# One-hot rows with the compared columns innermost in a four-layer graph network on one core

## The reference

```python
x = _layernorm(x + _L0_gnn_ref(x, src, dst, L0_gnn_W), axis=-1)      # mean over incoming edges
x = _layernorm(x + _L1_gnn_ref(x, edge_index, ...), axis=-1)         # sums over 16 neighbours of each node, twice
x = _layernorm(x + _L2_gnn_ref(x, ...), axis=-1)                     # attention over the edges
x = _layernorm(x + _L3_gnn_ref(batch0, src, dst, x, ...), axis=-1)

# in _L1: the neighbours of each node after a sort, deg = 16
order = jnp.lexsort((nbr, nodes))
nbrs = nbr[order].reshape(N, deg)
for k in range(deg):
    out = out + w[1 + k] * h[nbrs[:, k]]

# in _L3: how often each node is the source of an edge
deg_out = jax.ops.segment_sum(ones_e, src, num_segments=n)
norm_src = jax.lax.rsqrt(jnp.maximum(deg_out, 1.0))
```

## Time and profile before

| what | value |
|---|---|
| median of three runs | 10770.39 us |
| the profiled execution | 10772.08 us, of which 10770.3 us are the span of the profile |
| PE, DVE, ACT, POOL busy | 78%, 72%, 59%, 68% |
| the degree count (L564, L584, L587, L599) | ends at 512.7 us |
| mean layer and sort | about 540 to 2700 us |
| first window of layer 1 | about 2900 to 5540 us |
| second window of layer 1 | about 5550 to 6990 us |
| attention, last layer | 7000 us to the end |

### The profile page before, as it was taken

One profiled execution on the slowest core, in us unless ns is written; L12 is line 12 of the kernel. 1 busy time (PEld: TensorE's weight loads), 2 busy tenths in 40 slices (PEclk: granted clock), 3 DMA queues, 4 the chain that ended last, 5 costly groups with the idle time before them and its releaser, 6 DMA issues.

```text
span 10770.3 us, 189635 instructions
## 1 busy us (share of the span) xinstructions
PE 8431.4 (78%) x45271; PEld 6636.6 (62%) x45271; DVE 7796.5 (72%) x26977; ACT 6315.6 (59%) x18928; POOL 7356.1 (68%) x7060
## 2 busy tenths in 40 slices
PE   3344555555788999888889999989999999948987
PEld 2233444444466776677777878767777777736765
DVE  5678656655866777565654446788888888899999
ACT  6877777776856666111100004677777777756665
POOL 0076777777088888888838888466666666639995
PEclk6555555555889999999999999955555555557776
DMA  2021222222678888999967775221111111110000
GB/s 48 1 74 47 52 53 53 53 53 56 216 198 204 217 218 213 261 250 246 252 228 228 233 226 122 34 71 46 46 46 46 46 46 46 46 44 1 1 1 25
DMA packets 656017, 1170.97 MB, mean 109 GB/s; under 512 B 140942, under 2 KB 565074, under 8 KB 632158
## 3 DMA queue, kind: packets, MB, share of 16 engines
q0 software_dynamic: 363536, 437.35, 21.2%
q10 hardware_dynamic: 25344, 574.83, 13.9%
q1 hardware_dynamic: 266062, 146.67, 5.4%
HBM read 885.82 MB, written 278.99 MB: 108 GB/s over the span
## 4 chain that ended last, share of the span: by engine, by line
POOL 32%; DVE 19%; PE 18%; issue 14%; ACT 12%; DVEq 3%; DMA 2%; SPq 1%; ACTq 0%; POOLq 0%
POOL step_data L1404 12%; POOL onehot L2091 8%; PE bank L1365 7%; POOL step_data L1676 7%; POOL gather_ring L1404 4%; DVE step_small L1911 2%; DVE keys L1051 2%; ACT keys L584 2%; ACT onehot L980 2%; PE bank L1951 2%; DVE keys L1060 2%; PE bank L991 2%; ACT onehot L978 2%; DVE arena L1024 2%; PE bank_tile L1959 1%
## 5 line engine op out<-in xcount | busy, mean ns | idle before, releaser
L966 POOL DMA_INDIRECT gather_ring<-mean_rows,step_data x1660 | 1593.2, 960 | 951.3 <-DVE arena L763 396.9
L991 PE MATMUL bank<-gather_ring,onehot 128*128 128x130 f32 x3320 | 1045.6, 462 | 1050.8 <-DVE arena L1024 728.2
L1365 PE MATMUL bank<-arena 128*128 128x384 bf16 x9506 | 1796.6, 329 | 26.6 <-DMA arena<-split_out 24.8
L1365 PE MATMUL bank<-arena,keys 128*128 128x384 bf16 x9408 | 1791.6, 330 | 9.3 <-DMA arena<-split_im 9.3
L1404 POOL DMA_INDIRECT step_data<-hidden,window_idx x960 | 1554.9, 1620 | 315.9 <-issue 291.5
L991 PEld LDWEIGHTS bank<-gather_ring,onehot 128*128 128x128 f32 x3320 | 811.7, 309 | 1274.0 <-issue 853.5
L1365 PEld LDWEIGHTS bank<-arena 128*128 128x128 bf16 x9506 | 1306.9, 138 | 328.1 <-issue 39.8
L1365 PEld LDWEIGHTS bank<-arena,keys 128*128 128x128 bf16 x9408 | 1294.2, 138 | 317.8 <-issue 34.5
L1676 POOL DMA_INDIRECT step_data<-next_rows,window_idx x672 | 1117.3, 1663 | 343.7 <-issue 314.6
L1882 POOL DMA_INDIRECT gather_ring<-attention_rows,step_data x834 | 786.1, 943 | 606.7 <-DVE step_small L1935 459.5
L1882 POOL DMA_INDIRECT keys<-attention_rows,step_data x826 | 778.4, 942 | 468.3 <-DVE step_small L1935 420.3
(11 more groups left out here) (361 smaller groups left out, 22016.6 us busy)
## 6 DMA issues: line engine op xcount, KB each, us to landing
keys<-count_rows ACTq DMA_DIRECT2D x56, 3136.0 KB, 11.6
arena<-count_rows ACTq DMA_DIRECT2D x56, 3136.0 KB, 11.4
count_rows<-arena ACTq DMA_DIRECT2D x29, 3136.0 KB
count_rows<-keys ACTq DMA_DIRECT2D x29, 3136.0 KB
gather_ring<-mean_rows,step_data POOLq DMA_INDIRECT x1660, 2.5
step_data<-hidden,window_idx POOLq DMA_INDIRECT x960
gather_ring<-attention_rows,step_data POOLq DMA_INDIRECT x834, 2.5
keys<-attention_rows,step_data POOLq DMA_INDIRECT x826, 2.5
```

Source lines behind the costliest of these rows:

```text
L966: e.indirect_dma_start(ring_at(rings.slot(name, i), SUM_COLS, SUMS - 1), None, rows, bass.IndirectOffsetOnAxis(src_idx[:, i:i + 1], 0), bo ...
L991: e.matmul(pass_bank[i % N_SUM_BANKS][:, 0:SUMS], onehot[:, i % STEP_SLOTS, :], ring_at(rings.slot(name, i), SUM_COLS, SUMS), start=True, ...
L1365: m = e.matmul(pass_bank[n % 2][:, 0:SPLIT_COLS], counts[t % 2][:, :, h], split[:, h, :], start=(h == 0), stop=(h == NODE_TILES - 1))
```

## The change

Both kinds of one-hot tables turn their two inner dimensions: the column (or group) is now the innermost one. What was `[slot][column][value]` is `[slot][value][column]`, and `low_hot` goes from `[group][value]` to `[value][group]`. For this the comparison needs an iota in which each value stands 8 or 4 times in a row: `iota_wide` (128 x 8) and `iota_quad` (128 x 4), two copies made once at the start. In the comparison before, the digits were an operand whose innermost step is 0 (one digit repeated 98 or 128 times). Now the digits run innermost with step 1 and are repeated by an outer dimension, and the iota is read plainly. The results of a comparison are written as one contiguous run, as before.

The other users of the tables now step through them. ACT's eight writes of a group (L584) go to every eighth element, 16 bytes apart, and PE reads both operands of the degree count with that step. For the count matrices, PE reads its stationary operand in steps of 4 elements, 8 bytes. ACT's relu still runs over all 1024 elements at once.

Last, `far` names 1 group out of 4 rather than 3 out of 5, which makes 50 groups of low one-hots on ACT rather than 120, and 150 on DVE rather than 80. All of ACT's groups (0, 4, 8, ...) now lie in slot 0 of the ring.

```diff
+    iota_quad = sb("iota_quad", [P, P, HOT_GROUPS], BF16)
...
     low_hot = [onehot[:, 4 + 2 * i:6 + 2 * i, :].rearrange("p s e -> p (s e)").bitcast(BF16).rearrange(
-        "p (g e) -> p g e", e=P) for i in range(2)]
+        "p (e g) -> p e g", g=HOT_GROUPS) for i in range(2)]
...
-        "p (s c w) -> p s c w", s=HIST_SLOTS, c=HIST_COLS) for at, w in ((0, NODE_TILES), (2 * LANE // 4, P)))
+        "p (s w c) -> p s w c", s=HIST_SLOTS, c=HIST_COLS) for at, w in ((0, NODE_TILES), (2 * LANE // 4, P)))
+    iota_wide = acc[:, 60 * P:60 * P + P * HIST_COLS // 2].bitcast(BF16).rearrange("p (w c) -> p w c", c=HIST_COLS)
...
     def far(i):
-        return i % 5 in (0, 2, 4)
+        return i % 4 == 0
...
                 e.tensor_tensor(to[:, s, :, :],
-                                of[:, cols].rearrange("p (c o) -> p c o", o=1).to_broadcast(
-                                    [LOAD_PARTS, HIST_COLS, width]),
-                                iota_half[0:LOAD_PARTS, 0:width].rearrange("p (o w) -> p o w", o=1).to_broadcast(
-                                    [LOAD_PARTS, HIST_COLS, width]), ALU.is_equal).then_inc(made)
+                                of[:, cols].rearrange("p (o c) -> p o c", o=1).to_broadcast(
+                                    [LOAD_PARTS, width, HIST_COLS]),
+                                iota_wide[0:LOAD_PARTS, 0:width, :], ALU.is_equal).then_inc(made)
...
-                    e.activation(to[:, c, :], iota_half[0:LOAD_PARTS, :], ACT.Abs, bias=low_digit[:, at:at + 1],
+                    e.activation(to[:, :, c], iota_half[0:LOAD_PARTS, :], ACT.Abs, bias=low_digit[:, at:at + 1],
                                  scale=-1.0).then_inc(hist_far)
...
-                m = e.matmul(hist, low_store[:, s, c, :], high_store[:, s, c, :], start=(i == c == 0),
+                m = e.matmul(hist, low_store[:, s, :, c], high_store[:, s, :, c], start=(i == c == 0),
...
+        own().tensor_copy(iota_wide[:, :, :], iota_half[:, :].rearrange("p (w o) -> p w o", o=1).to_broadcast(
+            [P, P, HIST_COLS])).then_inc(n.sem, n.up())
+        own().tensor_copy(iota_quad[:, :, :], iota_half[:, :].rearrange("p (w o) -> p w o", o=1).to_broadcast(
+            [P, P, HOT_GROUPS])).then_inc(n.sem, n.up())
...
-                low_code[t % 2][:, g:g + HOT_GROUPS].rearrange("p (c o) -> p c o", o=1).to_broadcast([P, HOT_GROUPS, P]),
-                iota_half[:, :].rearrange("p (o w) -> p o w", o=1).to_broadcast([P, HOT_GROUPS, P]),
+                low_code[t % 2][:, g:g + HOT_GROUPS].rearrange("p (o c) -> p o c", o=1).to_broadcast([P, P, HOT_GROUPS]),
+                iota_quad[:, :, :],
                 ALU.is_equal).then_inc(lows_made)
...
-        e.matmul(count_bank[b % 4][:, 0:GROUP_COLS], low_hot[c % 2][:, i, :], high_hot[b >= ROUND][c % 2][:, i, :],
+        e.matmul(count_bank[b % 4][:, 0:GROUP_COLS], low_hot[c % 2][:, :, i], high_hot[b >= ROUND][c % 2][:, i, :],
```

## The result

The changed kernel takes 10706.8 us (median of four runs, 10704.28 to 10712.14), against 10770.15 (median of four, 10768.21 to 10776.99) on the same chip: a ratio of 0.9941, with a 95% interval of 0.9923 to 0.9958. It is 63 us faster. Forecast were 171 us and a time of 10599. The direction was right, the size was not, and the time lies above the range of 10560 to 10690.

A forecast was written before the change was run, and what follows sets the result against it. ACT was taken to bound the degree count, gathers the first window of layer 1. Savings of 151 us (count) and 20 us (gathers) made 171 us, so 10599 us; forecast 10565 to 10635, range 10560 to 10690.

The forecast's parts named there:

- What bounds the kernel: Degree count: ACT alone is the chain, 99.3%, with serial work behind; layer 1's first window: gathers; DVE bounds neither window.
- DVE's durations: Comparisons of 784, 1024 and 512 elements were to take about 0.56, 0.68 and 0.43 us.
- The lower end: New DVE comparison: 0.52 ns an element, from one-source rows of 4-byte elements; the upper end was today's 1.042.
- The edge-row loop: Degree count's start, taken to hang on DVE: 16.6 us less, so ACT's next group starts at 154.0 us.
- The turn: Degree count: ACT's group and PE's matmuls in series, 5.13 us per four groups; 40 turns, count ends at 361.3 us.
- Two costs of it no row shows directly: 16-byte steps in the degree count: ACT's write +40 ns an Abs, PE's read +25 ns a matmul.
- the steps bind: Rival: 16-byte writes and reads cost their upper ends, turn 6.65 us, 111 us less, 10659 us; chance 0.22.
- DVE doesn't get faster: Rival: comparisons stay at 1.042 ns an element, DVE bounds the degree count, 49 us less, 10721 us; chance 0.06.
- The slower case: Rival: the quick comparison holds up layer 1's gathers more, 26 us slower in all, 10796 us; chance 0.04.
- The gathers: First window of layer 1: shorter comparison cuts gather delays of at most 54 us by 38%; 20 us taken.
- PE's weight load: Count matrices: stationary operand's load may grow from 98 to 138 ns, hidden behind matmuls of 384 columns; price 0.

The follow-up runs named there:

- e4: Changed kernel, but PE reads both operands of the degree count as contiguous runs (counts come out wrong): 11244.94 us, count to 438.6 us.
- e11: Changed kernel with 8-byte steps as in e2, and ACT making the low one-hots of 1 group in 5: 11191.95 us, 0.9822 of the kernel before.
- e2: Changed kernel with all low one-hots on DVE and a group's columns in two blocks of four (8-byte steps): 11145.95 us, 0.9822 of the kernel before.
- e5: Kernel before with the count-matrix part alone (low_hot turned, iota_quad): 11320.51 us, 0.9977 of the kernel before.
- e7: Kernel before with the count-matrix part alone, plus a memset of 240 elements behind each low comparison: 11316.74 us, 0.9979 of the kernel before.
- e8: Kernel before with the new share alone (far names 1 group in 4), old layouts: 11292.75 us, 0.9954 of the kernel before.
- e1: Changed kernel, but DVE makes all low one-hots of the degree count and ACT none: 11205.27 us, 0.9876 of the kernel before.
- e9: Changed kernel, but PE reads only the stationary operand of the degree count contiguously (counts come out wrong): 11325.02 us, count to 481.4 us.
- e3: Changed kernel, but each ACT Abs writes 128 elements in a row (source degrees come out wrong): 11200.38 us, count to 395.8 us.
- e6: Kernel before with the count-matrix part alone, each low comparison made twice: 11332.46 us, 0.9989 of the kernel before.
- e10: Changed kernel, but PE reads only the moving operand of the degree count contiguously (counts come out wrong): 11297.06 us, count to 446.4 us.

## Why the prediction went wrong

**What bounds the kernel**: right. ACT alone paced the degree count, and nothing hides behind it: ACT's, PE's and DVE's share there changed and the rest moved along (mean layer 2147 us in both).

**DVE's durations**: right. 566, 685 and 425 ns were measured, about 560, 680 and 430 forecast. The lower end (0.52 ns an element, from the 4-byte rows) was the one to take: from 784 to 1024 elements it is now (685 - 566) / 240 = 0.50 ns an element, where it was 1.042. With this the trace agrees with both halves of the rule on two 16-bit tensors in the Trainium skill, "VectorE: DVE Perf Modes", section "Mode 2×_1P".

**The edge-row loop**: wrong by 10.2 us. I let it hang on DVE (16.6 us less), but a PE group of 1.45 us instead of 0.65 fills its rounds: 24 matmuls and three transposes are 5.4 of 5.9 us. In e4, with contiguous reads, ACT's first group after the loop starts at 155.4 us, near my 154.0; in the changed kernel at 164.16.

**The turn**: the failed step. Its form held (first Abs to relu's end, to PE, to the free slot). The passage "Two costs of it no row shows directly" chose +40 ns an Abs and +25 ns a matmul, with ends of +172 and +82. Measured were (4.97 - 2.43) / 8 = +318 ns and +100 ns: beyond both upper ends. The turn is therefore 2.22 us longer by ACT and 0.60 by PE than forecast, 7.94 instead of 5.13. The sum over 40 turns is 112 us; with the 10.2 of the loop and the 3.0 that are left for the tail, where PE's last three groups take 1.45 us each, not 0.7, it is the whole gap between 361.3 and 486.8 us.

What was wrong in the reasoning is that I read the cost as one that grows slowly with the length of the step, and placed 16 bytes near 8 because it is far from 196 and 528. The runs show a steep rise between 8 and 16 bytes instead:

| step of 2-byte elements | eight Abs of 128 (write) | distance of matmuls, 98 columns (moving read) |
|---|---|---|
| contiguous | 2.43 to 2.45 us | 81 to 83 ns |
| 8 bytes | 2.63 us (e11) | 91 ns (e11), 0.89 us for eight (e2) |
| 16 bytes | 4.83 to 4.97 us | 175 to 181 ns |

The sentence of the Trainium skill, "Advanced Engine Details and Errata", section "SBUF Cachelines", that I quoted against my sum (lines of 16 bytes, a penalty for a new line at every access) also says that at least two hits on a line are needed to absorb the latency. A step of 8 bytes gives two hits, one of 16 gives one. The table agrees with that on both sides. No run has a step between 8 and 16 bytes or, for these two accesses, one above 16, so where the rise lies and whether it goes on is not shown. I read the rule, gave it no price and left the price at the nearest row, which was on the other side of the rise. L1839, with a step of 528 bytes on DVE, showed 1.35 ns an element; ACT's Abs at 16 bytes pays 0.32 us / 128 = 2.5 ns. An end taken from DVE's rows was no bound for ACT.

**The rivals**: "the steps bind" was the right mechanism, with 0.22. It was priced at a turn of 6.65 us, from ends that were too low. "DVE doesn't get faster" gave 10721 us, near the measured time, by another road; the durations refute it. The slower case did not come: from 3400 to 4200 us gathers come every 800 / 442 = 1.81 us, where it was 1.85.

**The gathers**: right in kind, too small in size. Forecast 20 us in the first window, from delays that shrink in proportion to the comparison (38% of 54 us). They shrank by more, as the table of e5 to e7 shows: 0.039 us a gather, 30 us for 765 of them. Measured 38 there and 10 in the second on the first chip; e5, which holds that part alone, is 25 us faster in all (11345.52 to 11320.51), and its window of 2625.4 us is 20 us shorter than e8's 2645.0. Some of the 38 may be what windows vary by between kernels that differ only in the degree count: e1 to e4 and e9 to e11 have 2616 to 2629. I had left the second window's gathers out.

**PE's weight load** of the count matrices was priced at nothing, and that was right: it grew from 98 to 113 ns, and the second window's matmuls come as densely as before, 2350 in 380 us (2337 in the earlier trace rows). A move of 8 bytes again, and cheap.

```profile
L1356 PEld LDWEIGHTS bank_tile<-keys,onehot 128*128 128x128 bf16 x928 | 104.7, 113 | 101.2 <-issue 69.1 <-ACT arena L1362 8.0 <-ACT keys L1362 2.2
```

## A version that beats both

e2 does: 8-byte steps and all low one-hots on DVE, 0.9822 of the kernel before, where the changed kernel is at 0.9941 on its chip. The count ends at 332.1 us instead of 486.8. e11 has the same ratio on its own chip and ends the count 8 us later, so giving ACT a share gains nothing.

## What to carry to other kernels

A layout that makes a comparison faster is paid for by everyone who reads or writes across it: count those accesses first. In this kernel a step of 8 bytes was cheap for 2-byte elements and one of 16 was not. Where a cost is unknown, ask whether it can rise steeply between the nearest row and yours, and let a stated rule widen the range; two ends taken from rows of other engines are no bounds. When a stage has two costs in series in one turn, removing each in turn shows what it costs, and removing the helper (ACT here) may beat both. An operation that is held only by what was under way when it began loses more than in proportion when that grows longer.

## What the runs showed of the hardware that was not expected

- A step of 16 bytes doubles the distance of matmuls of 98 columns when it is in the moving operand (175 to 181 ns against 81 to 83), and the time of an ACT write (4.97 us against 2.43 for eight), for 2-byte elements; one of 8 bytes adds about 11% and 8%.
- Neither distance follows TensorE's clock. With the step, PE is busy without a gap in e1 and in e3 and makes the same 886 matmuls in 160 us, at a granted clock of 1.00 and of 0.50:

```profile
170.00:330.00 160.00, 160.00 (x886) 128.33 (x885) 129.00 (x222) 0.00 (x0) 0.00 (x0) 1.00 0.00 1
```

```profile
170.00:330.00 160.00, 160.00 (x886) 128.32 (x884) 112.44 (x194) 99.52 (x251) 0.00 (x0) 0.50 0.00 1
```

  Without it, the kernel before and e6, whose degree counts have the same code, are equally fast at 0.50 and at 1.00; 16 matmuls take 1.46 us in the earlier trace rows and in e6:

```profile
170.00:330.00 160.00, 55.97 (x599) 47.45 (x598) 101.62 (x103) 158.14 (x411) 0.00 (x0) 0.50 0.00 1
```

```profile
170.00:330.00 160.00, 56.12 (x600) 47.76 (x600) 103.99 (x105) 158.47 (x410) 0.00 (x0) 1.00 0.00 1
302.06 1.46 PE L601 MATMUL bank<-keys 125*128 125x98 bf16 x16 [2.70 <-ACT keys L589]
```

  In both pairs PE is equally busy at either clock; what set the clock is open.
- The stationary operand hides the same step almost wholly. Alone it costs nothing that the distance shows (e10: 82 ns, though its weight load takes 161 ns where it takes 142 in e4), and beside the moving operand's step 6 ns (e9: 175 against 181).
- A gather of GpSimd is held only by the comparison of two tensors under which it begins, for what is left of that less 0.13 us; one that starts later doesn't hold it, and the gather doesn't hold the comparison (before, e5 to e8).
